# Loads of sample 2 issued ahead of the weight of sample 0, and two transposes on VectorE placed earlier in the prologue

## The reference

```python
# L0: adapter, weights chosen by the first id
h = relu(x @ W1[lang] + b1[lang])             # 512 -> 128
y = x + (h @ W2[lang] + b2[lang])             # 128 -> 512
x = x + layernorm(y) * gamma[lang] + beta[lang]
# L1: conditional linear layer, weights chosen by the second id
x = x + (x @ W[cat] + b[cat])                 # 512 -> 512
```

## Time and profile before

| | before |
|---|---|
| median of 3 runs | 615.1 us (613.81 to 616.61) |
| profiled execution, its own time | 614.85 us |
| span of its instructions | 613.0 us |
| PE busy | 606.5 us, 99% |
| DVE busy | 520.0 us, 85% |
| ACT busy | 512.9 us, 84% |
| POOL busy | 520.9 us, 85% |
| granted TensorE clock | 1.00 |

### The profile page before, as it was taken

One profiled execution on the slowest core, in us unless ns is written; L12 is line 12 of the kernel. 1 busy time (PEld: TensorE's weight loads), 2 busy tenths in 40 slices (PEclk: granted clock), 3 DMA queues, 4 the chain that ended last, 5 costly groups with the idle time before them and its releaser, 6 DMA issues.

```text
span 613.0 us, 10710 instructions
## 1 busy us (share of the span) xinstructions
PE 606.5 (99%) x2863; PEld 488.4 (80%) x2863; DVE 520.0 (85%) x1151; ACT 512.9 (84%) x770; POOL 520.9 (85%) x263
## 2 busy tenths in 40 slices
PE   9999999999999999999999999999999999999998
PEld 7676787778888877787888888888888888888887
DVE  1799979889899889898888899899898889898673
ACT  4878888889888889889989889889888889889770
POOL 6778889899888899889999898899888899889830
PEclk9999999999999999999999999999999999999999
DMA  8989799887998898899898998888898898998422
GB/s 302 251 258 307 258 311 300 277 265 253 296 307 274 270 300 253 298 287 289 269 294 268 305 303 265 283 290 270 301 303 278 283 295 253 301 308 273 156 87 103
DMA packets 125938, 166.22 MB, mean 271 GB/s; under 512 B 11062, under 2 KB 72768, under 8 KB 121812
## 3 DMA queue, kind: packets, MB, share of 16 engines
q1 hardware_dynamic: 94900, 150.12, 75.2%
q10 hardware_dynamic: 30912, 15.73, 9.1%
q0 software_dynamic: 96, 0.05, 0.0%
HBM read 132.17 MB, written 33.55 MB: 270 GB/s over the span
## 4 chain that ended last, share of the span: by engine, by line
PE 75%; DMA 7%; ACT 6%; SPq 5%; DVE 3%; issue 3%; POOL 1%; ACTq 0%; DVEq 0%; POOLq 0%
PE o_bank L839 15%; PE o_bank L841 15%; PE o_bank L840 15%; PE n_bank L857 7%; DMA x_tok<-in_x 6%; PE d_bank L839 4%; PE d_bank L841 4%; PE d_bank L840 4%; PE d_bank L882 3%; ACT norm L501 2%; PE y_bank L839 2%; PE y_bank L841 2%; PE y_bank L840 2%; DVE x1T_lo L732 2%; DMA x_quad<-in_x 1%
## 5 line engine op out<-in xcount | busy, mean ns | idle before, releaser
L839 PE MATMUL o_bank<-w_hi,x1T_hi 128*128 128x512 f32 x512 | 205.6, 402 | 0.5 <-DVE x1T_lo L732 0.5
L841 PE MATMUL o_bank<-w_hi,x1T_lo 128*128 128x512 f32 x512 | 200.1, 391 | 0.0
L840 PE MATMUL o_bank<-w_lo,x1T_hi 128*128 128x512 f32 x512 | 199.1, 389 | 0.0
L428 POOL TENSOR_TENSOR w_lo<-w_raw,w_hi 128x1024 fp32r<-128x1024 f32 x62 | 149.1, 2404 | 10.0 <-ACT w_hi L511 9.8
L667 DVE STREAM_TRANSPOSE xT<-x_quad 128x512 f32<-128x512 f32 x120 | 127.2, 1101 | 34.1 <-DMA x_quad<-in_x 34.1
L501 ACT ACTIVATE norm<-y,neg_mean_rstd,rstd 128x512 f32<-128x512 f32 x128 | 152.2, 1266 | 1.1 <-DVE neg_mean_rstd L717 1.1
L423 POOL TENSOR_TENSOR x_tok<-x_tok,b_bc 128x1024 f32<-128x1024 f32 x60 | 145.0, 2416 | 5.4 <-DMA x_tok<-in_x 2.9
L518 ACT ACTIVATE x1T_hi<-n_bank,params 128x512 fp32r<-128x512 f32 x126 | 84.5, 688 | 34.7 <-DVE n_bank L726 29.5
L839 PEld LDWEIGHTS o_bank<-w_hi,x1T_hi 128*128 128x128 f32 x512 | 96.3, 188 | 21.1 <-issue 3.1
L841 PEld LDWEIGHTS o_bank<-w_hi,x1T_lo 128*128 128x128 f32 x512 | 96.1, 188 | 21.0
L840 PEld LDWEIGHTS o_bank<-w_lo,x1T_hi 128*128 128x128 f32 x512 | 96.4, 188 | 17.6
(11 more groups left out here) (95 smaller groups left out, 812.3 us busy)
## 6 DMA issues: line engine op xcount, KB each, us to landing
w_raw<-in_L_cond_W SPq DMA_DIRECT2D x32, 1024.0 KB, 6.6
out<-out_half SPq DMA_DIRECT2D x63, 512.0 KB, 4.5
x_tok<-in_x SPq DMA_DIRECT2D x31, 1024.0 KB, 11.4
w_raw<-in_L_cond_W SPq DMA_DIRECT2D x64, 256.0 KB, 4.3
b_bc<-in_L_cond_b SPq DMA_DIRECT2D x64, 256.0 KB, 8.7
x_quad<-in_x SPq DMA_DIRECT2D x62, 256.0 KB, 3.8
x_quad<-in_x ACTq DMA_DIRECT2D x58, 256.0 KB, 10.7
x_tok<-in_x ACTq DMA_DIRECT2D x2, 256.0 KB, 3.3
```

Of the source, the lines that this page charges most:

```text
L428: pool.tensor_tensor(w_lo[q][:, c:c + 2, :], w_raw[q][:, c:c + 2, :], w_hi[q][:, c:c + 2, :].bitcast(F32), ALU.subtract).then_inc(w_lo_don ...
L839: pe.matmul(acc, lhs_hi, rhs_hi, start=first, stop=False)
L840: pe.matmul(acc, lhs_hi, rhs_lo, start=False, stop=False)
L841: return pe.matmul(acc, lhs_lo, rhs_hi, start=False, stop=last)
```

## The change

SP issues the four quarters of sample 2 ahead of the wait for the ids, and so ahead of W of sample 0 and of b1 of sample 1. On DVE the first transpose of sample 2 stands ahead of the statistics of sample 0, with a wait for the eight copies of ACT ahead of it, so that `xT_done` is counted in order; the second transpose stands ahead of `low_h(k1)` instead of behind it.

```diff
@@ SP, prologue
             load_b2(lang1, 1)
             load_w1(lang1, 1)
             load_w2(lang1, 1)
+            load_x_quads(2, 0, range(NQ))
             sp.wait_ge(cat_in, 16)
             load_w(sample_id(1, 0, G), 0)
             sp.dma_start(params[1][:, 2 * NC:NP], b1[bass.ds(lang1, 1)].rearrange("o a -> a o")
                          ).then_inc(first_b1_in[1], 16)
-            load_x_quads(2, 0, range(NQ))
             sp.wait_ge(table_done, 1)
@@ DVE, prologue
             for t in range(NT):
                 y_tile(k0, t)
                 mean(k0, t)
+            dve.wait_ge(xT_done, 2 * NC)
+            turn_next_x(k1, 0)
             variance(k0)
             inverse_deviation(k0)
-            turn_next_x(k1, 0)
+            turn_next_x(k1, 1)
             low_h(k1)
-            turn_next_x(k1, 1)
             y_pair(k1, 0)
             y_pair(k1, 1)
```

## The result

The changed kernel takes 617.86 us (median of 7 runs, 616.70 to 621.99) where the kernel before takes 613.45 us (7 runs beside it): ratio 1.0079, interval 1.0051 to 1.0107. That is 4 to 5 us slower. I had forecast about one us slower, "no change", and a range to 617.6; the time lies outside it and the change of 0.8% is clear of noise.

A forecast was written before the change was run, and what follows sets the result against it. PE was taken as the bound, busy without a gap from 50 us, so only that stretch's start could move. Relu +2.0, ACT's slack -0.93, DVE's gain 0 gave +1.1 us: 616.0 us, range 613.8 to 617.6.

The forecast's parts named there:

- Step 2: SP's queue: b1 of sample 1 lands behind W at 22.5 us, so its first relu waits 2.0 us.
- s: How much later the first relu of sample 1 starts on ACT than 20.55 us: 2.0 us forecast.
- step 1: SP's queue: with order swapped, quarters land at 18.9 us instead of 22.4 and W at 22.4 instead of 17.9.
- Step 5: ACT's order behind the relu: a late relu less 0.93 us of slack makes x1T_hi 1.07 us later.
- my slack of 0.93: ACT's idle time between relu and x1T_hi, 0.17 + 0.76 us, taken to absorb part of a late relu.
- Step 3: GpSimd's identity addition to W ends at 24.0 us, before ACT's split wants it at 24.56: no cost.
- Step 4: DVE's two turns come earlier; low(h) could gain 1.2 us, but the late relu covers that: gain 0.
- The second: Rival: SP's issue of W is held until the quarters land, b1 at 25.5, end 4.0 us later; chance 0.05.
- The first: Rival: b1 lands on time, before 21.5 us, and DVE's gain comes, about -0.9 us; chance 0.22.
- the third: Rival: W and quarters together last less when swapped, b1 at 21.5, slack absorbs it, 0.0 to 0.1 us; chance 0.13.

The follow-up runs named there:

- SP's part alone: Changed kernel with DVE's order put back as before, so only the order of SP's loads is changed: 618.73 us, ratio 1.0098.
- the clock held up: Changed kernel with 30 instead of 10 idle products on PE behind the up projection of sample 1: 616.87 us, ratio 1.0065.
- b1 alone moved: Kernel before with b1 of sample 1 issued behind the four quarters instead of ahead of them, W still ahead: 615.19 us, ratio 1.0033.
- the two kernels in which b1 doesn't hide it: Changed kernel with b1 of sample 1 issued ahead of the quarters (613.65 us, 1.0009), or between quarters and W (614.30 us, 1.0005).
- the kernel without that hold: Changed kernel whose four loads of sample 2 write 32 partitions each in pieces of 8 KB instead of 512 B: 616.15 us, ratio 1.0055.

## Why the prediction was wrong

*Step 2, the wait for b1.* Right in kind: the load that the diff doesn't name lands behind W, the relu waits for it, and the whole measured loss hangs on this wait (moved forward alone, the load brings 1.0079 down to 1.0009). Wrong in size, and this is the step that failed: s = 2.0 us predicted, 4.84 measured (20.55 to 25.39). It failed because step 1 priced each load by its share in the old order and kept those shares. The quarters' own 4.5 us held (20.2 - 15.7). W2, which used to run beside loads to all partitions, landed 1.3 us later, and W, which now runs beside the tail of the quarters and the next sample's loads, took 4.8 instead of 3.5. Those two are 2.6 of the 2.84 us. In the other two profiles with this order of loads s was 3.4 (SP's part alone) and 5.6 (the clock held up): the term was too small each time, by an amount that varies from one execution to the next. The trace of the kernel before held a warning. Its windows while W and while the quarters were at work:

```profile
13.00:16.00 3.00, 2.75 (x16) 2.24 (x16) 1.62 (x5) 2.71 (x6) 2.94 (x3) 1.00 1.04 408
16.00:19.00 3.00, 3.00 (x10) 1.69 (x9) 2.34 (x10) 2.97 (x7) 3.00 (x4) 1.00 1.21 226
```

W then ran at 408 GB/s beside loads to all partitions, the quarters at 226. My 4.5 us for the quarters hold that slow rate already; what the rows don't say is what a neighbour loses beside it, and I put that at nothing without asking.

*Step 5, ACT's chain.* Right: a relu s late costs s less about one us (with b1 alone moved, 2.54 gave 1.40; my slack of 0.93 was 1.14). With s = 4.84 that is 3.7 to 3.9.

*The missing term: the clock.* The prediction doesn't speak of PE's pause or of its clock. With low(h) at 23.9, as it had it, the pause would have ended near 24.6. At 4.7 us of pause the clock fell, and the second projection became the later branch into x1T_hi. What is left of the 5.30 us after ACT's 3.7 to 3.9 is 1.4 to 1.6; the kernel with the clock held, which measures it apart, gives 1.6. With both terms taken from those other kernels the sum closes: 4.84 - 1.14 + 1.6 = 5.3, which is what PE's start shows.

*Step 3, W late at no cost.* Shown only behind b1. In the two kernels in which b1 doesn't hide it, PE's start was 0.1 and 1.3 us later, with W landed at 24.1 and 25.3; the medians (1.0009 and 1.0005) show no cost.

*Step 4, DVE.* Right: turn, statistics, turn in 3.1 us (3.4 in the prediction), with the statistics done at 22.4 hidden by the late relu. Its gain of 1.2 us needed quarters at 18.9; they came at 20.2. The row at 18.29 that the prediction read as the end of the means is the first instruction of the statistics (line 700); nothing hung on it, since the turn waited for the quarters.

*The rivals.* The second had the size (b1 at 25.5, +4.0) by luck, with the wrong mechanism: W's issue did take 2.83 us, but it was let go at 15.5 and not when the quarters had landed (20.2), and the kernel without that hold landed W at 24.4. The first and the third did not occur. The range ended at one more us for b1, and the three terms that I missed all point the same way. The chance of 0.04 for slower was too small for a sum whose largest term was read off another order.

## What to carry to other kernels

When a load is moved ahead in a queue, list every load it overtakes, and look first at the smallest: someone may wait for it, and it costs nothing to issue it earlier. A transfer's share of a queue is not its own, and changes with what runs beside it: read the GB/s of its window, and where loads write few partitions, as the quarters do, leave room for what runs beside and behind them to land later. Read a landing from more than one execution: that of b1 moved by over 2 us between profiles with the same order of loads. A new wait that pauses PE for some us should be priced once more with the products behind it at half the clock (0.43 us apart here instead of 0.23).

## What the runs showed of the hardware that was not expected

While four loads of 256 KB to 32 partitions each were at work, the core's DMAs moved 221 to 252 GB/s, whether in pieces of 512 B or 8 KB; with the same bytes to 128 partitions they moved 353 to 419. Pieces of 512 B and of 2 KB to 128 partitions were close: 353 and 388 GB/s beside 419 and 365. A load of 0.5 KB took 9.7 and 13.4 us to land when it was issued behind the quarters and W, 1 MB each. With a pause of PE of 4.7 us the clock fell to 1.2 GHz for the products behind it, and 20 more idle products in it kept the clock at 0.999 or 1.000 in six of six runs. Pauses of 3.17 and 3.23 us stood before no fall in one profile and before a fall in another.
